# Scatter stage of a graph network: bucket marks made for four tiles by one bf16 comparison, and first lanes read from a table instead of registers

## The reference

```python
h = jnp.maximum(_layernorm(x, axis=-1), 0.0)
x = x + _L0_gnn_ref(h, src, dst, edge_weight, L0_gnn_weight, L0_gnn_gamma, L0_gnn_beta)
...
support = x @ hamilton                       # in _L0_gnn_ref; edge_row = src, edge_col = dst
msg = edge_val[:, None] * support[edge_col]
out = jax.ops.segment_sum(msg, edge_row, num_segments=x.shape[0])
```

## Time and profile before

| what | us |
|---|---|
| median of 3 runs | 9156.01 (9151.04 to 9163.85) |
| the profiled execution's own time | 9157.83 |
| its span, first to last instruction | 9156.1 |
| `place` (L926), first to last start | 266.9 to 2722.4 |
| POOL's record writes (L1103), first to last start | 321.0 to 2743.5 |

### The profile page before, as it was taken

One profiled execution on the slowest core, in us unless ns is written; L12 is line 12 of the kernel. 1 busy time (PEld: TensorE's weight loads), 2 busy tenths in 40 slices (PEclk: granted clock), 3 DMA queues, 4 the chain that ended last, 5 costly groups with the idle time before them and its releaser, 6 DMA issues. The chain is left out here.

```text
span 9156.1 us, 186469 instructions
## 1 busy us (share of the span) xinstructions
PE 6298.5 (69%) x35446; PEld 4950.7 (54%) x35447; DVE 6016.1 (66%) x19386; ACT 2528.7 (28%) x8033; POOL 4862.9 (53%) x4975
## 2 busy tenths in 40 slices
PE   1677777777765745556665355688658888888886
PEld 1566666666664533335555222466546666666664
DVE  8566666666658965558887888899744444444444
ACT  5345545454541132221110222111022222122222
POOL 0466666666666410007776000377437777777773
PEclk9555555555555655558887555799865555555556
DMA  6644444444445649997778699866733333333333
GB/s 132 144 140 137 139 136 137 138 139 139 136 124 107 139 91 195 195 183 226 227 230 189 163 258 256 207 183 185 125 98 81 81 81 81 81 81 80 82 81 30
DMA packets 1820630, 1294.78 MB, mean 141 GB/s; under 512 B 1262518, under 2 KB 1641558, under 8 KB 1818560
## 3 DMA queue, kind: packets, MB, share of 16 engines
q1 hardware_dynamic: 1578096, 840.20, 39.3%
q0 software_dynamic: 200704, 415.20, 17.4%
q10 hardware_dynamic: 40912, 29.67, 1.5%
HBM read 922.86 MB, written 361.78 MB: 140 GB/s over the span
## 5 line engine op out<-in xcount | busy, mean ns | idle before, releaser
L1103 POOL DMA_INDIRECT sorted_edges<-arena,idx x1664 | 1622.8, 975 | 946.0 <-issue 621.5
L2218 POOL DMA_INDIRECT arena<-node_table,idx x1760 | 1660.7, 944 | 557.0 <-issue 385.5
L1018 PE MATMUL banks<-arena,edge_tables 128*128 x3520 | 1173.3, 441 | 527.8 <-DVE edge_tables L954 513.7
L1018 PEld LDWEIGHTS banks<-arena,edge_tables 128*128 128x128 f32 x3520 | 900.6, 318 | 663.6 <-issue 615.4
L2194 PE MATMUL banks<-arena 128*128 128x64 f32 x3520 | 1215.1, 449 | 0.0
L1604 PE MATMUL banks<-arena 128*128 x3520 | 671.6, 361 | 766.9 <-issue 463.4
L2189 PE MATMUL banks<-arena 128*64 128x65 f32 x3520 | 844.2, 343 | 400.3 <-ACT arena L2205 399.9
L2093 POOL DMA_INDIRECT arena<-expanded,idx x576 | 544.6, 945 | 1006.2 <-DVE idx L1970 789.5
L2194 PEld LDWEIGHTS banks<-arena 128*128 128x128 f32 x3520 | 884.6, 312 | 211.3
L2205 ACT ACTIVATE arena<-arena 128x64 f32<-128x64 f32 x1760 | 449.9, 257 | 1788.3 <-DVE arena L2157 1782.8
L2164 DVE TENSOR_TENSOR arena<-arena,banks 128x64 f32 x1760 | 388.1, 220 | 844.7 <-PE banks L2194 820.7
(11 more groups left out here) (423 smaller groups left out, 11905.3 us busy)
## 6 DMA issues: line engine op xcount, KB each, us to landing
arena<-sorted_edges SPq DMA_DIRECT2D x220, 524.0 KB
arena<-lanes_dram SPq DMA_DIRECT2D x222, 512.0 KB, 8.0
expanded<-arena SPq DMA_DIRECT2D x110, 784.0 KB, 8.0
arena<-in_attr_rows SPq DMA_DIRECT2D x576, 130.0 KB
arena<-sorted_edges SPq DMA_DIRECT2D x110, 536.0 KB
arena<-row_keys SPq DMA_DIRECT2D x110, 512.0 KB, 4.9
arena<-sorted_edges SPq DMA_DIRECT2D x110, 512.0 KB, 5.6
expanded<-arena SPq DMA_DIRECT2D x110, 512.0 KB, 6.6
```

The source lines that it names most:

```text
L1018: nc.tensor.matmul(m.psum[j % 4][:, 0:D], m.onehot[:, j % 4, :], m.support[:, bass.ds(blocks[j] * D, D)], start=True, stop=True).then_inc( ...
L1103: nc.gpsimd.indirect_dma_start(m.sorted, bass.IndirectOffsetOnAxis(ap=m.idx[:, j % (4 * CH):j % (4 * CH) + 1], axis=0), m.out_ring[:, slot ...
L2218: nc.gpsimd.indirect_dma_start(slots[:, j % SLOTS, 0:D], None, m.table, bass.IndirectOffsetOnAxis(ap=m.idx[:, j % SLOTS:j % SLOTS + 1], ax ...
```

## The change

The marks get a layout in which the four tiles of a quad lie side by side for each bucket (`p q f s`, s = 4), so PE reads one tile's marks with a step of four bf16 elements. One TENSOR_TENSOR comparison of 396 elements makes a quad's marks, from a table of bucket numbers repeated four times (`numbers4`) and the tile's bucket numbers narrowed to bf16 once per round (`narrow`). The first lanes of a round's 128 steps are computed once per round (`know`) from 128 block numbers that SP copies to all partitions by a DMA. The DVE register load of the block numbers goes; that of the slots stays. Some small tables are put into one allocation, `per_node`, which then holds marks, `numbers4` and `bucket16` during the stage.

```diff
+    m.numbers4 = per_node[:, 0:at].bitcast(BF16).rearrange("p (f s) -> p f s", s=4)
+    m.bucket16 = per_node[:, at:at + RING // 2].bitcast(BF16)
+    m.marks = per_node[:, at:at + 4 * BUCKETS].bitcast(BF16).rearrange("p (q f s) -> p q f s", q=2, s=4)
...
+        blocks_in, first_lane = m.scale_row[:, 0:RING].bitcast(I32), m.shift_row[:, 0:RING]
...
+            def blocks(i, first=0):
+                sp.dma_start(blocks_in[:, first:RING],
+                             m.plan_rows[0, bass.ds(i * RING + LAG + first, RING - first)].partition_broadcast(P)
+                             ).then_inc(s["blocks_in"], 16)
...
+                if more and c == 1:
+                    sp.wait_ge(s["blocks_known"], i + 2)
+                    settle(sp)
+                    blocks(i + 1)
...
-                def mark(j):
-
-                    n = i * RING + j
-                    v.tensor_scalar(m.marks[:, j % 4, 0:BUCKETS], m.iota16[:, 0:BUCKETS], m.bucket[:, bass.ds(n, 1)], None, ALU.is_equal
-                                    ).then_inc(s["marked"], 1)
+                def know(first=0):
+
+                    dve.wait_ge(s["blocks_in"], i * 16 + 32)
+                    v.tensor_scalar(first_lane[:, first:RING], blocks_in[:, first:RING], float(P), m.lane_no[:, :], ALU.mult, ALU.add
+                                    ).then_inc(s["blocks_known"], 1)
+                    dve.wait_ge(s["blocks_known"], i + 2)
+
+                def narrow():
+
+                    v.tensor_copy(bucket16, m.bucket[:, bass.ds(i * RING, RING)]).then_inc(s["narrow"], 1)
+                    dve.wait_ge(s["narrow"], i + 1)
+
+                def mark(q):
+
+                    v.tensor_tensor(m.marks[:, q % 2, 0:BUCKETS, :], numbers4,
+                                    bucket16[:, q * QUAD:(q + 1) * QUAD].unsqueeze(1).to_broadcast([P, BUCKETS, QUAD]),
+                                    ALU.is_equal).then_inc(s["marked"], 1)
...
-                        for to, row, most in ((blocks, 0, SPARE - 1), (slots, 2, RING - 1)):
-                            to.update(enumerate(group(nc, ENG.DVE, m.plan, row, k, most), j))
+                        slots.update(enumerate(group(nc, ENG.DVE, m.plan, 2, k, RING - 1), j))
...
-                                    m.block_part[:, bass.ds(blocks[j], 1)], None, ALU.is_equal).then_inc(s["onehot"], 1)
+                                    first_lane[:, j:j + 1], None, ALU.is_equal).then_inc(s["onehot"], 1)
...
+                know(first)
+                if ranks:
+                    narrow()
+                    mark(0)
                 for j in range(first, RING + 2):
-                    if ranks and j == 0:
-                        mark(0)
-                    if ranks and j + 1 < RING:
-                        mark(j + 1)
+                    if ranks and j % QUAD == 1 and j // QUAD + 1 < quads:
+                        mark(j // QUAD + 1)
...
-                pe.wait_ge(s["marked"], n + 1)
+                if j % QUAD == 0:
+                    pe.wait_ge(s["marked"], i * quads + j // QUAD + 1)
                 pe.wait_ge(s["placed"], n + 1)
-                nc.tensor.matmul(rank, m.from16[:, :], m.marks[:, (j + 3) % 4, 0:BUCKETS], start=False, stop=False,
+                nc.tensor.matmul(rank, m.from16[:, :], marks_of(j - 1), start=False, stop=False,
                                  skip_group_check=True)
```

More of the change, by code:

```diff
@@ L254, in allocate @@
     at += 2 * P
-    m.marks = tables[:, at:at + 2 * SPARE].bitcast(BF16).rearrange("p (a f) -> p a f", f=SPARE)
-    at += 2 * SPARE
     m.below = tables[:, at:at + 4 * SPARE].bitcast(BF16).rearrange("p (a f) -> p a f", f=SPARE)
-    assert at + 4 * SPARE == 4 * TP + SCRATCH
+    assert at + 4 * SPARE <= 4 * TP + SCRATCH
     m.gram = sb("gram", [D, RW])
@@ L276, in allocate @@
     m.block_part = sb("block_part", [P, SPARE])
[L277 to L281, removed]
+    per_node = sb("per_node", [P, 4 * NB + 6 * D])
+    m.dout, m.din, m.stat, m.stat2 = (per_node[:, n * NB:(n + 1) * NB] for n in range(4))
+    m.small = per_node[:, 4 * NB:4 * NB + 6 * D]
+    at = 2 * BUCKETS
+    m.numbers4 = per_node[:, 0:at].bitcast(BF16).rearrange("p (f s) -> p f s", s=4)
+    m.bucket16 = per_node[:, at:at + RING // 2].bitcast(BF16)
+    at += RING // 2
+    m.marks = per_node[:, at:at + 4 * BUCKETS].bitcast(BF16).rearrange("p (q f s) -> p q f s", q=2, s=4)
+    assert at + 4 * BUCKETS <= 4 * NB + 6 * D
     m.w = {n: sb(f"w_{n}", [P, P]) for n in WEIGHTS}
@@ L834, in scatter_by_source @@
         scattered = ring(nc, "scattered", 2 * CH)
-        s |= sems(nc, "filled", "rows_stored", "rows_back")
+        s |= sems(nc, "filled", "rows_stored", "rows_back", "blocks_in", "blocks_known", "narrow")
+        blocks_in, first_lane = m.scale_row[:, 0:RING].bitcast(I32), m.shift_row[:, 0:RING]
+        numbers4, bucket16 = m.numbers4, m.bucket16
         sorted_tiles = m.sorted.rearrange("(p t) f -> p t f", p=P)
@@ L874, in both @@
                              attr_tiles[:, bass.ds(i * RING + (c + 2) * CH, CH), :]).then_inc(rec_attr[h], 16)
+            blocks(-1, RING - LAG)
             for c in range(CHUNKS):
                 rows(0, c)
+            sp.wait_ge(s["blocks_known"], 1)
+            blocks(0)
             for c in range(2):
@@ L890, in _ @@
             for c in range(CHUNKS - 2):
-                both(ROUNDS - 1, c)
+                both(ROUNDS - 1, c, False)
             for c in range(CHUNKS):
@@ L903, in _ @@
             v.tensor_copy(rank, m.counters[:, :]).then_inc(s["blank"], 1)
-            dve.wait_ge(s["blank"], 4)
+            v.tensor_copy(numbers4, m.iota_row[:, 0:BUCKETS].unsqueeze(2).to_broadcast([P, BUCKETS, QUAD])).then_inc(s["blank"], 1)
+            v.memset(m.marks.rearrange("p q f s -> p (q f s)"), 0.0).then_inc(s["blank"], 1)
+            dve.wait_ge(s["blank"], 6)
             v.sem_inc(s["cleared"], quads)
@@ L990, in _, with marks_of @@
             opened.then_inc(s["opened"], 1)
-            pe.wait_ge(s["blank"], 4)
+            pe.wait_ge(s["blank"], 6)
+            def marks_of(j):
+                return m.marks[:, j // QUAD % 2, 0:BUCKETS, j % QUAD]
             def count(i, j):
                 n = i * RING + j
-                pe.wait_ge(s["marked"], n + 1)
+                if j % QUAD == 0:
+                    pe.wait_ge(s["marked"], i * quads + j // QUAD + 1)
                 pe.wait_ge(s["placed"], n + 1)
-                nc.tensor.matmul(rank, m.from16[:, :], m.marks[:, (j + 3) % 4, 0:BUCKETS], start=False, stop=False,
+                nc.tensor.matmul(rank, m.from16[:, :], marks_of(j - 1), start=False, stop=False,
                                  skip_group_check=True)
-                nc.tensor.matmul(rank, m.upto16[:, :], m.marks[:, j % 4, 0:BUCKETS], start=False, stop=False,
+                nc.tensor.matmul(rank, m.upto16[:, :], marks_of(j), start=False, stop=False,
                                  skip_group_check=True).then_inc(s["ranked"], 1)
@@ L1003, in count @@
                     pe.wait_ge(s["below"], n + QUAD)
-                nc.tensor.matmul(upto_block[0:BUCKETS, :], m.marks[:, j % 4, 0:BUCKETS], m.below[:, j % 8, 0:BUCKETS], start=False, stop=False,
+                nc.tensor.matmul(upto_block[0:BUCKETS, :], marks_of(j), m.below[:, j % 8, 0:BUCKETS], start=False, stop=False,
                                  skip_group_check=True).then_inc(s["held"], 1)
```

7 lines of the change are left out of this document (3 added, 4 removed).

## The result

| kernel | median, us | runs | profiled span, us |
|---|---|---|---|
| before | 9157.03 | 4 (9151.04 to 9163.85) | 9156.1 |
| after | 8928.72 | 4 (8922.76 to 8932.55) | 8920.1 |

The ratio is 0.975, with a 95% interval of 0.9733 to 0.9767. The forecast was 8960 us; the time lies 31 us under it, inside the range. The lines have moved: the mark is now L945, `place` L955, `match` L982, the two counts L1033 and L1035, the product of the one-hot L1053, the pairs L1063, POOL's writes L1138, the register loads L801.

What follows compares the result with a forecast made beforehand. DVE's steps were taken to bound the scatter stage, with POOL 311 us behind. Register load -208, ordinary loop 0 and round starts +10 gave -198 us on 9157.8, so 8960 us, range 8895 to 9010 (chance 0.68).

Steps and rivals of the forecast that it cites:

- What bounds the stage: In `scatter_by_source`, DVE's steps set the pace; POOL is 311 us behind, its writes alone needing 2113 us.
- The register load: DVE steps with loads: one load fewer shortens each by 1.00 us, 208 steps, -208 us (bounds -171 and -229).
- The ordinary loop: DVE-PE loop in ten of 16 steps: edits cancel, sum about 0 (bounds -60 and +83 us).
- the quad's mark: DVE, one ordinary step of four: the mark makes the step 0.93 us, 0.07 over the old; 403 steps, +28 us.
- The -42 us for marks that were held up: Old marks on DVE are held up at times; removing them saves 1664 x 0.025 us where they are on the path.
- The forecast's count of steps, 403 and 624: Ordinary steps: 403 make a quad's mark (+28 us), the other 624 pay 0.02 us each (+12 us).
- The pair steps: Steps where PE multiplies attribute pairs: PE sets the time, both `place` starts shift alike, the difference stays.
- The start of a round: `know`, `narrow` and the first mark run in sequence: 0.8 us, 13 times, +10 us (bounds 0 and +20).
- Strided marks: Rival: PE reads marks with 8-byte step at half rate, 0.083 us per matmul, +276 us, 9236 us; chance 0.06.
- The mark collides with POOL: Rival: each of 416 new marks on DVE waits half a POOL write, 0.49 us, +204 us, 9164 us; chance 0.05.
- POOL becomes the bound: Rival: steps shorten more than thought and POOL's own 2113 us hold, 8847 us; chance 0.10.
- The register wait costs all of its bound: Rival: `place` waiting for ranks through a register operation costs the full +83 us, 9043 us; chance 0.11.

Runs made afterwards that it cites:

- the run with the fixed column: The changed kernel, with `place` reading its bucket number from a fixed column filled by one more copy a round: 8861.51 us, ratio 0.9688.
- The table alone: The kernel before with first lanes from the table and one register load per eight steps, old marks kept: 8935.18 us, ratio 0.9739.
- the loads put apart: The kernel before with its two register loads per eight steps four steps from each other, marks as before: 9119.73 us, ratio 0.9966.
- The run with the moved mark: The changed kernel with the quad's mark made in the quad's fourth step, the pair step, instead of the second: 8935.21 us, ratio 0.9738.
- the packed marks: The changed kernel with each tile's marks packed by itself, DVE writing with a step of 99 elements: 9509.41 us, ratio 1.0402.
- the marks alone: The changed kernel with both rows in register loads again, `know` and its DMA left out: 9227.63 us, ratio 1.0053.

## Why the prediction was right, and where it was off

**What bounds the stage**: right. DVE's steps set the pace, POOL followed by 222.5 us, and in the run with the fixed column POOL took over at 2133 us, forecast 2113.

**The register load**: the mechanism is right, the size was too small, -208 against -258 us. Taking a load away (1.00 us a step) also made the other one 0.21 us shorter; 208 x 0.213 = 44 us, most of the miss. The forecast took the remaining load at the 0.82 us of this stage. The trace before had the short load too: in a later stage, whose loop loads one row on DVE, eight values at a time, the line of the loads is

```profile
L800 DVEq TENSOR_LOAD <-target_plan x220: 594/597/653, 6802.8 to 9013.4; - x110
```

The table alone shows the effect without the marks, the loads put apart show that adjacency isn't the cause. What is, stays open.

**The ordinary loop**: off, 0 against +73 us, near the upper bound of +83, and for reasons that the bound didn't have. The run with the moved mark parts them: its ten ordinary steps sum to 9.27 us and its four pair steps to 7.05.
- The loop's own terms: the register operation on the rank's wait +0.117 us by the run with the fixed column (forecast 0.08); PE's missing wait -0.089 (0.472 to 0.383 us from `place` to the first count; forecast -0.06); between the counts +0.029, forecast nothing, of which the step explains 0.009. In sum the undisturbed loop went from 0.836 to 0.888 us, +0.05 (forecast +0.02), which is 54 us in 1040 steps.
- The step of the forecast that failed is the quad's mark. It was booked on DVE's own row, 0.07 us in the step that makes it. The step that makes it has room (0.90 us in the median). The price comes on PE one step later, 1.06 us: the mark holds `match`, `match` holds its product, and the next count is queued behind that. In the ordinary steps this is 104 x (9.72 - 9.27) = 47 us; the pair steps give 104 x (7.05 - 6.84) = 22 us of it back.
- The -42 us for marks that were held up: what the ten ordinary steps take beyond ten of the shortest loop is 69 us before and 69 with the table alone, both with the old marks, and 41 with the moved mark. So some 28 us went with the old marks. That it was their being held up is not shown.
- The forecast's count of steps, 403 and 624, leaves out 13 of the 1040: 0.3 us.

**The pair steps**: off, 0 against -42 us. The forecast said that both `place` starts shift alike. 22 of the 42 us are what the late step gives back. The other 20 are there with the moved mark too (7.24 to 7.05 us): the old mark stood ahead of every `match`, in the pair step too; now `match` starts 0.24 us after `place` in place of 0.40, and the products and the pairs behind it start earlier. Where `match` goes, PE follows, as long as PE is waiting for it.

**The start of a round**: right, +6 against +10 us.

**The rivals.** *Strided marks*: the price is 0.009 us a count, not 0.06, and the packed marks lose far more on DVE than they give on PE. By the section "Door 1: The DMA port swizzle" of the Trainium skill's page "SBUF — State Buffer" a step of 8 bytes costs nothing; the run agrees to 0.009 us. *The mark collides with POOL*: no mark is longer than 0.432 us while POOL is busy 370 of 500 us. This settles it better than the rows that the forecast used, which come from a stage in which POOL gathers (L1901) and doesn't write. The section "Who interferes with whom" on the same page of the Trainium skill gives its rule for a GpSimd instruction that reads SBUF; it also says that a `tensor_tensor` was not seen to stall a DMA issued by GpSimd. POOL's writes agree with that remark, 971 ns in the median before and after. In the other direction, 416 marks show no wait for a write's end. *POOL becomes the bound*: not in this kernel, but in the next edit. *The register wait costs all of its bound*: it costs more than the 0.10 us assumed there, and PE's saved wait covers most of it.

The errors of the terms are -50, +73, -42 and -4 us, -23 in sum, and 13 us less were spent beyond the stage. Their sizes are larger than their sum: the terms were less good than the time, and that the time came out so near is in part luck.

**What the change is worth by parts**: the table 2.6%, the marks nothing or a loss of 0.1 to 0.2% on top of it (0.9739 against 0.9750 and 0.9763, at the edge of what these runs can tell), 0.5% alone.

## What to carry to other kernels

Price an instruction that is put ahead of another on one engine by what that other one feeds: here a mark of 0.36 us cost next to nothing in its own step and 0.17 us on TensorE in the next. Then look one step further before the price is added up: 0.09 us of it came back there, because the one-hot that TensorE would have waited for was ready by then. A register operation that carries a wait on the critical loop cost 0.117 us each time here, and a copy into a fixed column once a round takes it away. When a kernel that undoes half of a change doesn't fit the sum of the parts, look at the loop's branch before the parts.

## What the runs showed of the hardware

- A load of eight values into DVE's registers takes 0.60 us where the loop loads one row on DVE (here, and in a later stage of the kernel before) and 0.82 us where it loads two, four steps apart or together.
- A bf16 comparison of 128x396 elements takes 0.360 us with neighbouring writes, and 2.015 us where consecutive writes lie 198 bytes apart: 5.1 ns an element.
- The loop's branch costs DVE 2.8 to 3.1 us in most rounds of the kernels before, after and with the table alone; with the marks alone there is a second pause of 2 to 3 us, at the branch or a few instructions behind it, and it moved when memsets were put ahead of the loop.
